# Last batch of an attention and feed-forward kernel: three small transfers of the denominators' chain issued from ScalarE's queue, the product one visit later

## The reference

```
x = x + attention(layernorm(x), ctx, ctx)      # 16 heads of 32
    q, k, v = (Q @ W_q.T, K @ W_k.T, V @ W_v.T) split into heads
    e = exp(clip(q k' / sqrt(32), -50, 50)), denom = sum(e)      # no maximum is subtracted
    out = ((e / denom) @ v) @ W_o.T
x = x + ffn(layernorm(x))                      # rows and weights rounded to int8 with absmax scales
```

## Time and profile before

| | |
|---|---|
| median of three runs | 1706.11 us |
| the profiled execution | 1705.6 us |
| its span in the profile | 1703.8 us |
| granted TensorE clock, mean | 0.999 |
| TensorE busy | 1671.9 us, 98% |
| VectorE busy | 1489.7 us, 87% |
| ScalarE busy | 1314.5 us, 77% |
| GpSimd busy | 133.7 us, 8% |
| final segments | 1330 to about 1672 us |

### The profile page before, as it was taken

The page is one execution under the profiler, slowest core; times in us unless marked ns, Lnnn a source line. Parts: engine busy times, 40 slices in busy tenths (PEclk is TensorE's granted clock), DMA queues, the critical chain, the costliest instruction groups (busy, mean ns, idle before and its releaser), DMA issues.

```text
span 1703.8 us, 29863 instructions
## 1 busy us (share of the span) xinstructions
PE 1671.9 (98%) x10418; PEld 1009.7 (59%) x10448; DVE 1489.7 (87%) x1705; ACT 1314.5 (77%) x1730; POOL 133.7 (8%) x75
## 2 busy tenths in 40 slices
PE   9999999999999999999999999999999999999998
PEld 8896655656565565656666566565656444444445
DVE  5657888888897989999898998989999889999997
ACT  5557788888887877877777787877878778788875
POOL 0000000000001111011110101111011000000001
PEclk9999999999999999999999999999999999999999
DMA  8687656566666566756657576566756799988971
GB/s 280 211 233 187 145 139 152 154 168 170 145 163 167 143 176 168 197 137 165 179 134 206 127 192 165 144 186 159 199 134 155 180 210 205 217 180 204 214 172 62
DMA packets 235059, 294.85 MB, mean 173 GB/s; under 512 B 28184, under 2 KB 142360, under 8 KB 234392
## 3 DMA queue, kind: packets, MB, share of 16 engines
q1 hardware_dynamic: 231688, 287.64, 66.5%
q10 hardware_dynamic: 3216, 5.24, 1.1%
HBM read 201.07 MB, written 91.48 MB: 172 GB/s over the span
## 4 chain that ended last, share of the span: by engine, by line
PE 82%; ACT 6%; DMA 5%; DVE 4%; issue 2%; SPq 1%; ACTq 0%; POOL 0%; POOLq 0%; DVEq 0%
PE wsum L999 25%; PE tile L962 24%; PE scores L984 21%; ACT probs L1247 5%; PE scores L1148 3%; PE scores L962 2%; DVE acc L1552 2%; PE tile L1148 1%; PE tile L1031 1%; DMA q_stack<-q_parts 1%; DMA row_lo<-o_parts 1%; DMA o_parts<-sums 1%; PE tile L1111 1%; DMA q_parts<-q_stack 1%; PE tile L1088 1%
## 5 line engine op out<-in xcount | busy, mean ns | idle before, releaser
L1247 ACT ACTIVATE probs<-scores 128x1024 f32<-128x1024 f32 x939 | 914.7, 1026 | 207.8 <-PE scores L984 169.3
L1552 DVE TENSOR_TENSOR acc<-acc,probs 128x2048 f32<-128x2048 f32 x439 | 1003.1, 2285 | 39.9 <-ACT probs L1247 25.3
L999 PE MATMUL wsum<-probs,v_sb 128*32 128x512 f32 x4096 | 492.4, 598 | 0.0
L984 PE MATMUL scores<-q_stack,k_stack 128*128 128x512 f32 x1536 | 444.5, 409 | 2.5 <-ACT probs L1247 1.7
L984 PEld LDWEIGHTS scores<-q_stack,k_stack 128*128 128x128 f32 x1536 | 264.9, 188 | 213.2 <-ACT probs L1247 121.3
L999 PEld LDWEIGHTS wsum<-probs,v_sb 128*32 128x32 f32 x4096 | 106.9, 109 | 243.9 <-issue 230.0
L1654 POOL TENSOR_TENSOR rstd<-var_eps,minus_half 128x1 f32<-128x1 f32 x48 | 105.9, 2207 | 1186.7 <-DVE var_eps L1446 1186.7
L1552 DVE TENSOR_TENSOR acc<-probs 128x2048 f32<-128x2048 f32 x32 | 73.4, 2293 | 56.7 <-PE tile L1031 51.2
L1148 PE MATMUL scores<-q_stack,k_stack 128*128 128x512 f32 x342 | 109.6, 421 | 8.6 <-ACT probs L1247 8.6
L962 PE MATMUL tile<-ctx_hi,wk_hi 128*128 128x256 f32 x412 | 116.4, 283 | 0.0
L962 PE MATMUL tile<-ctx_hi,wk_lo 128*128 128x256 f32 x412 | 116.0, 282 | 0.0
(11 more groups left out here) (255 smaller groups left out, 1988.4 us busy)
## 6 DMA issues: line engine op xcount, KB each, us to landing
k_stack<-k_parts SPq DMA_DIRECT2D x312, 256.0 KB, 7.8
q_stack<-q_parts SPq DMA_DIRECT2D x124, 256.0 KB, 7.2
v_sb<-v_parts SPq DMA_DIRECT2D x80, 256.0 KB, 7.5
v_parts<-v_stage SPq DMA_DIRECT2D x64, 256.0 KB, 5.0
raw<-ctxT SPq DMA_DIRECT2D x27, 512.0 KB, 5.6
k_parts<-stage_hi SPq DMA_DIRECT2D x96, 128.0 KB, 4.7
k_parts<-stage_lo SPq DMA_DIRECT2D x96, 128.0 KB, 2.5
x_in<-x SPq DMA_DIRECT2D x33, 256.0 KB, 4.2
```

What stands on the lines that cost most here:

```text
L984: last = nc.tensor.matmul(scores[:, h, :], k_stack[:, kt // 4, h, (kt % 4) * P:(kt % 4 + 1) * P], q_stack[:, qb, h, :], start=True, stop=True)
L999: last = nc.tensor.matmul(wsum[DH * h:DH * h + DH, :], v_sb[:, kt, DH * h:DH * h + DH], probs[:, n % RING, h, :], start=(kt == 0), stop=(k ...
L1247: nc.scalar.activation(probs[:, slot % RING, 2 * pair:2 * pair + 2, :], score_banks(seg, slot, pair), ACT.Exp, scale=1.0 / math.sqrt(DH)). ...
L1552: nc.vector.tensor_tensor(acc[:, :, :], other, probs[:, slot % RING, :, :], ALU.add).then_inc(sems["add_done"], 1)
```

## The change

In the final segments alone, SyncE no longer issues the three DMAs of the chain. ScalarE does: the spread at the end of visit 0, right behind the copy of the denominators (it waits for that copy), the store at the end of visit 4 (it waits for the reciprocals), the broadcast at the end of visit 6 (it waits for the store). VectorE's product goes from the end of visit 6 to the end of visit 8. The cast, the low part and the stores of the result stay where they were.

```diff
@@ chain (SyncE)
-                    if slot == first + (1 if seg.final else 2):
+                    if slot == first + 2 and not seg.final:
                         ct.wait_alone(sp, "denoms_copied", k)
                         sp.dma_start(den_c[:, :], denoms[0:P:DH, :]).then_inc(sems["denoms_spread"], 16)
-                    if slot == first + 4:
+                    if slot == first + 4 and not seg.final:
                         ct.wait_alone(sp, "recips_ready", k)
                         sp.dma_start(recip_row.rearrange("h (a j) -> (h a) j", j=G * QB // P), recip_c[:, :]).then_inc(sems["recips_stored"], 16)
-                    if slot == first + 5:
+                    if slot == first + 5 and not seg.final:
                         ct.wait_alone(sp, "recips_stored", 16 * k)
                         sp.dma_start(denoms[:, :], recip_row[:, None, :].broadcast_to((G, DH, QB))) \
                             .then_inc(sems["recips_loaded"], 16)
@@ end of a visit (ScalarE), behind half_done
+                    if seg.final:
+                        k = even // KT
+                        if even % KT == 0:
+                            ct.wait(act, "denoms_copied", k + 1 - 1)
+                            act.dma_start(den_c[:, :], denoms[0:P:DH, :]).then_inc(sems["denoms_spread"], 16)
+                        if even % KT == 4:
+                            ct.wait(act, "recips_ready", k)
+                            act.dma_start(recip_row.rearrange("h (a j) -> (h a) j", j=G * QB // P), recip_c[:, :]).then_inc(sems["recips_stored"], 16)
+                        if even % KT == 6:
+                            ct.wait(act, "recips_stored", 16 * k)
+                            act.dma_start(denoms[:, :], recip_row[:, None, :].broadcast_to((G, DH, QB))).then_inc(sems["recips_loaded"], 16)
@@ product (VectorE)
-                        if on and even == first + (6 if seg.final else 8):
+                        if on and even == first + 8:
```

## The result

The changed kernel takes 1741.44 us (median of four runs, 1739.01 to 1747.64) where the kernel before takes 1706.28 us (four runs): ratio 1.021 (95% interval 1.0192 to 1.0227; the brackets behind later ratios are such intervals), 35 us slower. The forecast was 1713.0 us, in a range of 1706 to 1720: the direction was right, and the size off by five times. The profiled execution took 1739.01 us, its span 1736.9 us, 33.1 us more than before.

The account below looks back on a forecast made before the run. It took ScalarE's first exponential of a visit, awaited by TensorE, as the bound. 4.85 + 0 + 3.60 - 1.5 = 6.95, say 6.9 us, on 1705.6 gave 1712.5, put at 1713.0 us for the runs; range 1706 to 1720.

Parts of the forecast that it names:

- The bound: Final segments: TensorE and ScalarE form a ring of 4.37 us per visit; a late first exponential delays the kernel equally.
- Step 1: Spread issued behind ScalarE's copy, eight halves: next exponential about 0.65 us later in seven, 0.3 in one; 4.85 us.
- that rival: At the spread on ScalarE: exponential starts during the issue, leaving only the hand-over, 0.4 us; 1709.2 us, chance 0.10.
- Step 2: Store and broadcast issued by ScalarE, eight times each, beside the second exponential: 0 us, upper bound 6.8.
- Step 3: VectorE's product one visit later: ScalarE's cast and visit 12's first exponential late in three halves; 3.60 us.
- the sum: Added delays from the product's later place in three halves, 1.90, 0.90 and 0.80: 3.60 us.
- Step 4: SyncE without the chain's waits issues loads sooner; TensorE's wait for the queries goes: -1.5 us, bounds 0 and -3.0.
- The rival of slowed issues: A full DMA system lengthens ScalarE's issues, adding 9.1 us: 1722 us; chance of half way there or more 0.14.
- The sum's own range: Whole forecast, 1713.0 us, with each term said to be half way to its bounds: 1709.5 to 1717 us.

## Why the prediction was wrong, point by point

- **The bound** was right: TensorE waits for ScalarE's first exponential of a visit, and what came was more of that wait, 30.7 us.
- **Step 1, the spread, 4.85 us**, was right: 0.63 to 0.75 us more behind the copy in seven halves, 1.25 in the first, and 4.3 us in all when moved alone (interval 2.6 to 6.0). The exponential isn't queued past the issue, so that rival is out.
- **Step 2, store and broadcast at 0**, was right for the issues, 0.32 and 0.54 us. It missed that ScalarE also waits for reciprocals and store to land before it may issue; I gave the store a visit of 4.4 us, and it took up to 8.7. The cost is 6.4 us of waits in one half of the profiled execution, and 9.9 us in four places in the run with everything a visit later and the spread back on SyncE.
- **Step 3, 3.60 us**, is the step that failed. The product's place alone cost 4.8 us (2.7 to 6.5) in an experiment, near the sum, though the cast waited in six halves there and not in three. But the sum stood on a condition, "this holds if the broadcast has landed", and I had its 7.6 us from a queue in which it was issued ahead of the loads. The change puts it behind them: 11.4 to 17.3 us where it was waited for, and 20.7 us of waits of the cast. Holding the loads back gave 24 us back.
- Beside it I drew on the Trainium skill (DMA: Bandwidth & Descriptors, Queues, rings and completion order), by which each DMA engine takes turns between queue rows, and inferred an earlier landing on ScalarE's own row. The traces don't bear that inference out: among the loads, the broadcast of the same half took 14.1 us on ScalarE's row and 13.6 us on SyncE's.
- **Step 4, -1.5 us**: the wait for the queries went as forecast. But I counted the earlier loads as a gain and put their price at nothing, without a reason. They are what made step 3 fail. I also counted 72 us of waits that leave SyncE's queue and overlooked a third, 15.9 us for the landing of the store. "Nobody had waited for them" was true of those who need the loads; who shares the DMA engines with them was not asked.
- **The rival of slowed issues**, 1722 us, was near in size and wrong in kind: only one of the 24 issues passed 0.78 us (it took 1.13); it was the landing that slowed. That its 1722 us came nearest is luck.
- A fall of TensorE's clock was in no term. The windows with its single waits of 3.6 to 6.6 us had a mean granted clock of 0.93 to 0.96, those with none over 1.5 us 1.00, but for one of 0.97 right behind such a wait. Matmuls were busy 5.3 us longer.
- The sum's own range doesn't come out of its terms: each of them half way to its bounds gives about 1708 to 1718.5 us, not 1709.5 to 1717. The result lies far above either.

## What to carry to other kernels

A wait in a queue that issues DMAs is also a brake on all that stands behind it. Who takes one away must ask what goes out earlier and which awaited transfer it will then precede: not only who needs the loads, but who shares the DMA engines with them. A landing time holds for its place among the other transfers, so it isn't to be taken over when the order changes; and, as the runs here have it, a small transfer that someone waits for goes out ahead of the bulk, from whatever queue.

## What the runs showed of the hardware

- A queue of its own gave a small transfer no way past the bulk: the store of 8 KB from ScalarE's queue landed after 1.4 us in the best case and 8.7 us in the worst, with loads of 256 KB each from SyncE's queue under way. The broadcast took 14.1 us from ScalarE's queue and 13.6 us from SyncE's, in the same half and behind the same kind of loads.
- The broadcast of 256 KB took 4.9 to 6.7 us to land with the loads held back, 7.4 to 7.6 us with the loads right behind it (where it was waited for in the kernel before), and 11.4 to 17.3 us among them. Issued among them as four DMAs of 32 partitions each, it cost 27 us less in all than as one.
- ScalarE's exponential behind its DMA issue started only when the issue was over: 0.68 to 0.75 us from the end of the copy with an issue of 0.53 to 0.60 us between, 1.29 us with one of 1.13 us, 0.05 us or less with none.
- Around and behind the end of a wait of 6.6 us TensorE's granted clock was 0.50 for 4 us, and 16 matmuls took 3.39 us that had taken 1.92 us at the full clock.
